# V quantised in a pipe over three engines, and K's parts and the ternary weights turned by the DMA crossbar

## What is computed

```python
kv = (cond @ Wkv + bkv).reshape(1, -1, 2, H, hd)      # cond: 4096 rows x 512, H = 16 heads of 32
k, v = kv[:, :, 0], kv[:, :, 1]
k = fq_sym(k, axis=-1)      # s = max|k| / 127 over a head's 32 columns; round(k / s) * s
v = fq_sym(v, axis=2)       # s = max|v| / 127 over all 4096 keys, for each column
# later: attn = softmax(q k^T), quantised to 0..255; out = attn v; projection; gated sum
# feed-forward: two products with weights w1, w2 that are round(w / mean|w|) clipped to -1..1
```

## Time and profile before

| | |
|---|---|
| three runs | 2114.99 us median, 2111.75 to 2115.88 |
| the profiled execution | 2113.4 us, of which the profiled span is 2111.6 |
| PE busy | 1680.1 us, 80% of the span |
| DVE | 1832.0 us, 87% |
| ACT | 1374.8 us, 65% |
| POOL | 1393.8 us, 66% |
| mean granted TensorE clock | 0.917 of full speed |

### The profile page before, as it was taken

The page is one execution under the profiler, slowest core; times in us unless marked ns, Lnnn a source line. Parts: engine busy times, 40 slices in busy tenths (PEclk is TensorE's granted clock), DMA queues, the critical chain, the costliest instruction groups (busy, mean ns, idle before and its releaser), DMA issues. The chain is left out here.

```text
span 2111.6 us, 38599 instructions
## 1 busy us (share of the span) xinstructions
PE 1680.1 (80%) x14322; PEld 855.0 (40%) x14336; DVE 1832.0 (87%) x2532; ACT 1374.8 (65%) x1294; POOL 1393.8 (66%) x1693
## 2 busy tenths in 40 slices
PE   7899999158888888888888878878878878753546
PEld 3455555014444444444444434434434434322223
DVE  6798888869999989989989989979989956648887
ACT  4344444147877877877877877867877852387771
POOL 0022222438998988988988988988988985134431
PEclk9999999559999999999989999989999988886878
DMA  6533333247767777677667677677677663000001
GB/s 214 174 90 105 105 104 89 80 107 128 134 115 128 130 114 133 124 121 132 123 116 130 124 114 131 114 123 133 115 127 129 111 117 124 20 0 0 20 20 41
DMA packets 596911, 224.99 MB, mean 107 GB/s; under 512 B 537089, under 2 KB 570369, under 8 KB 594817
## 3 DMA queue, kind: packets, MB, share of 16 engines
q1 hardware_dynamic: 596160, 221.04, 51.9%
q0 software_dynamic: 576, 1.57, 0.2%
HBM read 65.27 MB, written 23.07 MB: 42 GB/s over the span
## 5 line engine op out<-in xcount | busy, mean ns | idle before, releaser
L750 DVE TENSOR_SCALAR_CACHE_REDUCE att_scaled<-att_scores,layer_nsq 128x1536 f32<-128x1536 f32 (+1 forms) x768 | 1202.6, 1634 | 91.9 <-PE att_scores L724 89.6
L796 ACT ACTIVATE att_pairs<-att_scaled,att_bias_row 128x4096 uint8<-128x4096 f32 x256 | 950.3, 3712 | 301.1 <-POOL att_bias_row L763 205.6
L772 POOL CAST att_probsT<-att_pairsT 128x1024 bf16<-128x1024 uint8 x1024 | 1022.7, 1042 | 82.1 <-DMA att_pairsT<-att_pairs 68.7
L724 PE MATMUL att_scores<-att_k_head,att_q_head 96*128 96x512 bf16 x2048 | 601.1, 398 | 154.1 <-DVE att_scaled L750 84.9
L711 PE MATMUL att_ps_o<-att_k_head,att_q_head 96*128 96x512 bf16 x1536 | 434.6, 394 | 80.4 <-ACT layer_o_sum L788 80.2
L724 PEld LDWEIGHTS att_scores<-att_k_head,att_q_head 96*128 96x128 bf16 x2048 | 167.2, 100 | 427.9 <-DVE att_scaled L750 242.5
L733 PEld LDWEIGHTS att_ps_o<-att_v_head,att_probsT 128*128 128x128 bf16 x8192 | 245.3, 96 | 67.0 <-issue 8.4
L711 PEld LDWEIGHTS att_ps_o<-att_k_head,att_q_head 96*128 96x128 bf16 x1536 | 147.7, 100 | 290.1 <-ACT layer_o_sum L788 119.7
L733 PE MATMUL att_ps_o<-att_v_head,att_probsT 128*128 128x32 bf16 x8192 | 246.4, 177 | 0.2 <-POOL att_probsT L772 0.2
L556 POOL TENSOR_TENSOR kv_rest<-kv_kq,kv_parts 128x512 f32<-128x512 f32 x32 | 37.9, 1185 | 195.7 <-ACT kv_parts L538 188.4
L760 POOL TENSOR_SCALAR att_low_row<-att_low 128x1 f32<-128x1 f32 x256 | 93.4, 365 | 61.2 <-DVE att_scaled L750 61.1
(11 more groups left out here) (143 smaller groups left out, 1683.6 us busy)
## 6 DMA issues: line engine op xcount, KB each, us to landing
k_parts<-kv_k_stage SPq DMA_DIRECT2D x16, 768.0 KB, 5.1
att_k_head<-k_parts SPq DMA_DIRECT2D x16, 768.0 KB, 6.5
q_w_in<-in_L_ffn_w_dram SPq DMA_DIRECT2D x32, 256.0 KB, 3.2
kv_weights_ctx_in<-in_ctx_dram SPq DMA_DIRECT2D x32, 256.0 KB, 4.1
kv_weights_w_in<-in_L_ffn_w_dram SPq DMA_DIRECT2D x32, 256.0 KB, 2.6
att_q_head<-q_ints SPq DMA_DIRECT2D x48, 128.0 KB, 6.3
q_x_in<-in_x_dram SPq DMA_DIRECT2D x16, 256.0 KB, 2.9
v_ints<-kv_v_int SPq DMA_DIRECT2D x4, 1024.0 KB, 5.2
```

The source lines that it names most:

```text
L724: last = pe.matmul(buffer[:, x:x + 512], q_head[slot][:, at:at + P], k_head[slot][:, STARTS[j] + x:STARTS[j] + x + 512], start=True, stop= ...
L750: dve.tensor_scalar(scaled[u][:, STARTS[j]:STARTS[j] + WIDTHS[j]], scores[(g * NCH + j) % 2][:, 0:WIDTHS[j]], kept["nsq"][:, g:g + 1], Non ...
L772: pool.tensor_copy(probsT[g % C_BUFS][:, parity * HALF + first:parity * HALF + first + HALF // 2, :] .rearrange("p k q -> p (k q)"), turne ...
L796: act.activation(pairs[g % R_BUFS][:, :].bitcast(U8).rearrange("p (c two) -> p two c", two=2), scaled[u][:, :].rearrange("p (two c) -> p t ...
```

## The change

It does three things, all within `project_keys_values`:

1. K's parts are turned by one DMA transpose per tile. `parts` has four slots for each head, the fourth filled with zeros, so that a tile is 128x2048 and each head's block of 128 columns comes out as 128 partitions. SP issues it in step k+4; the 16 TensorE transposes, their PSUM buffers and ScalarE's copies are gone. ScalarE's first cast of a tile waits until the crossbar has turned the tile that was in that buffer before.
2. The ternary weights are turned by one DMA transpose per piece, straight into `w1T` or `w2T`. The three steps that make them move from VectorE to GpSimd, between the `rest` and the third part of its step. SP's and GpSimd's programs are written out without loops. On VectorE the running minimum of V takes the place of the maximum of its negative.
3. V's integers: VectorE multiplies V by the inverse step in eight pieces of four tiles, ScalarE copies each to int8, GpSimd casts that to bf16 in head order into `v_int`.

```diff
-        parts = [c.sb(f"parts{i}", [P, H, 3, D], BF16) for i in range(2)]
+        parts = [c.sb(f"parts{i}", [P, H, 4, D], BF16) for i in range(2)]
+        PART = 4
+        v_round = [c.sb(f"v_round{i}", [P, PART, C], I8) for i in range(2)]
...
             @block.sync
+                sp.wait_ge(parts_padded, 2)
+                for g in range(KT + 6):
+                    if 2 <= g < KT:
+                        sp.wait_ge(ctx_turned, g - 1)
+                        sp.dma_start(ctx_in[g % 2][:, :], ctx_tiles[:, g, :]).then_inc(ctx_loaded[g % 2], 16)
...
+                        sp.wait_ge(tern_ready, g - 1)
+                        sp.dma_start(w_in[g % 2][:, :], piece).then_inc(w_loaded[g % 2], 16)
+                    if live(g - 2, KT):
+                        w = g - 2
...
+                        sp.wait_ge(tern_ready, w + 1)
+                        sp.dma_start_transpose(into, tern[w % 2][:, :]).then_inc(w_turned[w % 2], 16)
+                    if live(g - 4, KT):
+                        k = g - 4
+                        sp.wait_ge(parts_ready, k + 1)
+                        after(sp, k_stored[k // 2 % 2], 16 * (k // 4))
+                        sp.dma_start_transpose(k_stage[k // 2 % 2][:, :, k % 2 * P:(k % 2 + 1) * P],
+                                               parts[k % 2][:, :, :, :].rearrange("p h a d -> p (h a d)")).then_inc(parts_turned[k % 2], 16)
+                    if live(g - 5, KT) and (g - 5) % 2:
+                        k = (g - 5) // 2
+                        for i in range(2):
+                            sp.wait_ge(parts_turned[i], 16 * (k + 1))
...
             @block.tensor
-                    if live(g - 2, KT):
-                        after(pe, tern_ready, g - 1)
...
-                            last = pe.transpose(ps_w[s % 2][:, k, :], tern[s % 2][:, k * P:(k + 1) * P], kept["identb"][:, :])
...
-                    if live(g - 3, KT):
...
-                                last = pe.transpose(ps_t[half][0:3 * D, h % (H // 2), :],
-                                                    parts[r][:, h, :, :].rearrange("p a d -> p (a d)"), kept["identb"][:, :])
...
             @block.scalar
-                            act.copy(k_stage[r // 2][:, half * H // 2:(half + 1) * H // 2, (r % 2) * P:(r % 2 + 1) * P],
-                                     ps_t[half][0:3 * D, :, :]).then_inc(parts_kept, 1)
...
                         after(act, kv_math, NPER * (g - 1))
-                        after(act, parts_turned, 2 * (g - 3) if live(g - 3, KT) else 0)
+                        if live(g - 4, KT):
+                            act.wait_ge(parts_turned[r], 8 * (g - 4 - r) + 16)
                         act.copy(parts[r][:, :, 0, :], heads(kq[r][:, :])).then_inc(hi_ready, 1)
...
+                for i in range(KT // PART):
+                    act.wait_ge(v_norm, i + 1)
+                    after(act, v_int_ready, i - 1)
+                    act.copy(v_round[i % 2][:, :, :], v_raw[:, i * PART:(i + 1) * PART, :]).then_inc(v_rounded, 1)
...
             @block.gpsimd
                         pool.tensor_tensor(heads(rest[r][:, :]), heads(kq[r][:, :]), parts[r][:, :, 0, :],
                                            ALU.subtract).then_inc(rest_ready, 1)
+                    if live(g - 1, KT):
+                        r = (g - 1) % 2
+                        pool.wait_ge(w_loaded[r], 8 * (g - 1 - r) + 16)
+                        pool.tensor_scalar(w_in[r][:, :], w_in[r][:, :], kept["w_scale"][:, r:r + 1], ROUND,
+                                           ALU.mult, ALU.add).then_inc(w_math, 1)
+                        pool.wait_ge(w_math, 2 * g - 1)
+                        pool.tensor_scalar(w_in[r][:, :], w_in[r][:, :], ROUND + 1.0, ROUND - 1.0, ALU.min, ALU.max).then_inc(w_math, 1)
+                        pool.wait_ge(w_math, 2 * g)
+                        if live(g - 3, KT):
+                            pool.wait_ge(w_turned[r], 16 * ((g - 3) // 2 + 1))
+                        pool.tensor_scalar(tern[r][:, :], w_in[r][:, :], -ROUND, 1.0, ALU.add, ALU.mult).then_inc(tern_ready, 1)
                     if live(g - 2, KT):
                         after(pool, mid_ready, g - 1)
                         pool.tensor_tensor(parts[r][:, :, 2, :], heads(rest[r][:, :]), parts[r][:, :, 1, :],
                                            ALU.subtract).then_inc(parts_ready, 1)
...
+                    pool.tensor_copy(v_int[grp % 2][:, :, first:first + PART, :],
+                                     v_round[i % 2][:, :, :].rearrange("p j (h d) -> p h j d", d=D)).then_inc(v_int_ready, 1)
...
             @block.vector
-                        dve.scalar_tensor_tensor(v_low[:, :], v_tile, -1.0, v_low[:, :], ALU.mult, ALU.max).then_inc(kv_math, 1)
+                        dve.tensor_tensor(v_low[:, :], v_tile, v_low[:, :], ALU.min).then_inc(kv_math, 1)
...
-                    for j in range(GRP):
-                        dve.tensor_scalar(v_int[i % 2][:, :, j, :], heads(v_raw[:, i * GRP + j, :]), ROUND, -ROUND,
-                                          ALU.add, ALU.add).then_inc(v_int_ready, 1)
+                for i in range(KT // PART):
+                    block_ = v_raw[:, i * PART:(i + 1) * PART, :]
+                    dve.tensor_tensor(block_, block_, v_inv[:, :].unsqueeze(1).to_broadcast([P, PART, C]), ALU.mult).then_inc(v_norm, 1)
```

More of the change, by code:

```diff
@@ L12 @@
 U8 = mybir.dt.uint8
+I8 = mybir.dt.int8
 ALU = mybir.AluOpType
@@ L437, in _ @@
             def _(sp):
[L438 to L451, removed]
@@ L493, in step @@
                         last.then_inc(k_ready, 1)
-                    if live(g - 3, KT):
[L496 to L500, removed]
-                                last = pe.transpose(ps_t[half][0:3 * D, h % (H // 2), :],
-                                                    parts[r][:, h, :, :].rearrange("p a d -> p (a d)"), kept["identb"][:, :])
-                            last.then_inc(parts_turned, 1)
                 pipelined(pe, KT, UNROLL, 4, step)
@@ L514, in step @@
                         act.copy(inT[s % 2][:, :, :], ps_in[s % 2][:, :, :]).then_inc(ctx_kept, 1)
-                    if live(g - 4, KT):
-                        r = (s - 4) % 4
-                        if r % 2 == 0 and live(g - 8, KT):
-                            after(act, k_stored[r // 2], 4 * (g - r) - 16)
-                        for half in range(2):
-                            after(act, parts_turned, 2 * (g - 4) + half + 1)
-                            act.copy(k_stage[r // 2][:, half * H // 2:(half + 1) * H // 2, (r % 2) * P:(r % 2 + 1) * P],
-                                     ps_t[half][0:3 * D, :, :]).then_inc(parts_kept, 1)
-                    if live(g - 2, KT):
-                        r = (s - 2) % UNROLL
-                        after(act, w_turned, g - 1)
-                        if r % 2:
-                            act.copy(kept["w2T"][:, r // 2 * CT:(r // 2 + 1) * CT, ds((g - 2 - r) * (P // UNROLL), P)],
-                                     ps_w[s % 2][:, :, :]).then_inc(w_kept, 1)
-                        else:
-                            act.copy(kept["w1T"][:, :, ds((g - 2) * (P // 2), P)], ps_w[s % 2][:, :, :]).then_inc(w_kept, 1)
                     if live(g - 2, KT):
@@ L560, in step @@
                                            ALU.subtract).then_inc(parts_ready, 1)
-                pipelined(pool, KT, UNROLL, 4, step)
-                pool.wait_ge(v_math, 3)
-                for i in range(KT // GRP // 2, KT // GRP):
-                    block_ = v_raw[:, i * GRP:(i + 1) * GRP, :]
-                    pool.tensor_tensor(block_, block_, v_inv[:, :].unsqueeze(1).to_broadcast([P, GRP, C]), ALU.mult).then_inc(v_norm, 1)
+                for i in range(2):
+                    pool.memset(parts[i][:, :, 3, :], 0.0).then_inc(parts_padded, 1)
+                for g in range(KT + 2):
+                    step(g)
+                for i in range(KT // PART):
+                    grp, first = i * PART // GRP, i * PART % GRP
+                    pool.wait_ge(v_rounded, i + 1)
+                    after(pool, v_stored[grp % 2], 16 * (grp // 2))
+                    pool.tensor_copy(v_int[grp % 2][:, :, first:first + PART, :],
+                                     v_round[i % 2][:, :, :].rearrange("p j (h d) -> p h j d", d=D)).then_inc(v_int_ready, 1)
             @block.vector
```

52 lines of the change are left out of this document (19 added, 33 removed).

## The result

The changed kernel takes 2165.19 us (median of 4, 2160.05 to 2168.19) against 2114.26 us before: ratio 1.0237, 95% interval 1.0216 to 1.0258. It is slower by 51 us between the medians, where the forecast had 47. The profiled execution took 2166.59 us with a span of 2164.8 us, 53.2 more than the span of before.

The account below looks back on a forecast made before the run. The tile loop was taken as TensorE-bound before, and bound by a ring of waits through the crossbar transposes after: 2113.4 + 51 (ring) - 1 (start) + 2 (tile 30's end) - 5 (V) = 2160.4 us, range 2106 to 2218.

Parts of the forecast that it names:

- the ring: K/V tile loop: first part, remainder, weight steps, SP, two transposes, next first part; 10.5 us against 8.73, +51 us.
- The issue of the weight transpose: SP's issue of the 128x512 transpose in each tile: 0.74 us, bounds 0.33 and 1.97.
- GpSimd's weight steps: Three GpSimd tensor_scalar of 128x512 per tile: 0.61 us each and 0.09 before each, 2.10 in all.
- Port: In the tile loop, GpSimd's steps and VectorE's two-input steps shut each other out: 0.5 us a tile, bounds 0 and 2.8.
- Queueing and hand-overs: In the loop: cast to remainder 0.78, SP's wake 0.2, parts' transpose 4.3 plus 0.3 queueing, landing to ScalarE 0.1 us.
- Start, end of tile 30, V: Around the loop: first products earlier, -1 us; weight steps inside tile 30's end, +2; V's new pipe, -5.
- the third rival: Tile loop: ring of 12 us and TensorE's clock falls, 2205 to 2290 us; single falls mostly taken by slack; chance 0.13.
- TensorE's own work: Tile loop without both turns: 0.61 + 3.65 + 3.60 = 7.86 us of TensorE a tile.
- What the prediction said of the context load: Tile loop: not in the ring; lands 3.5 to 6.5 us after going out, so TensorE finishes before the ring comes round.
- The rival of the port that does not matter: Port no matter to one-input steps: ring 10.0 us, V gains 16, total 2135 us; chance 0.15.
- The rival of a ring that does not bind: Tile loop: ring 8.6 us or less, TensorE binds at about 8.1, total 2091 us, faster; chance 0.15.
- block by block: Crossbar turns a tile's 16 blocks one after the other: ring of 21 us or more, over 2450 us; chance 0.02.

## Why the prediction was right

2160.4 was forecast, in a range from 2106 to 2218, and 2165.2 measured. The mechanism was right. That the number is so near is in part luck: against the profiled execution (2166.6) the ring cost 10 us more than forecast, the start 1 more, V gained 2 more, and the untouched stages were 2.9 shorter, which leaves 6 of the 11. The steps:

- **The ring.** Right, and it is the whole result: ScalarE waits for the crossbar in the changed kernel, the period moves with each link that is taken out or put in (1.50 for 1.67, 0.55 for 0.74), and it opens with one DMA issued earlier. Forecast 10.5, measured 10.84; +51 against +61.4 us.
- **The issue of the weight transpose** is the term that was mis-sized. A quarter of the way between a plain issue and that of 16 blocks gave 0.74; it takes 1.19 to 1.20 at the median. The time does not go by blocks from a plain issue on: a plain issue takes 0.33, four blocks 1.19, sixteen 1.92 at the median. It stands in every turn of the ring: 29 x 0.45 = 13 us. With the 0.1 before the next issue, and a few issues that take up to 3.15 us, the link is 1.42 at the mean.
- **GpSimd's weight steps** were forecast at 0.61 from casts of other widths. Undisturbed they take 0.68, 0.61 and 0.62; the first, with a scale from SBUF, is the dearer.
- **Port.** 0.5 us were forecast. In the loop the means of the remainder and the three weight steps are 1308 (1152 at the least), 980 (680), 740 (614) and 670 (619) ns: 0.16 + 0.30 + 0.13 + 0.05 = 0.64.
- **Queueing and hand-overs** were too dear: 4.4 us from issue to landing at the median (4.6 forecast), 0.03 from ternary tile to SP (0.2 forecast), 0.69 from cast to remainder (0.78). They cancel about half of the three errors above; 0.3 us a tile are left.
- **Start, end of tile 30, V.** -0.1 (forecast -1), +2.1 (+2), -7.3 (-5). V gained more mostly since a cast of 2048 columns takes 1.89, not 2.1 (8 x 0.21 = 1.7 us).
- **TensorE's clock.** It fell in the loop (0.88 at the mean). From 150 us on about every second tile has an idle time of 3.9 to 6.6 us ahead of the context's turn, and its next eight products take 4.6 to 6.0 us instead of 3.60. TensorE's slack took that up, as the third rival said of single falls: `kq` was ready at least 2.8 us before every cast. With the order of one DMA changed and the same work the clock is 0.96, and of ScalarE's waits for the crossbar one of 0.3 us is left.
- **TensorE's own work** was put at 7.86 us a tile, by adding durations of rows that overlap (306.78 lies before 303.29 + 3.65 in rows 4). Where it waits for nothing in the kernel with the transpose first, its turns of the context start 7.31 us apart (256.45, 263.76). The sum does not hang on it, but the price of a ring that does not bind does: there VectorE, at 7.8, comes ahead of it.
- **What the prediction said of the context load** held in the changed kernel: it lands, and TensorE and VectorE do their work, before the ring comes round. That it binds as soon as the ring is open, it did not say, and two of my later expectations (four buffers, weights on VectorE) were missed by it.
- **The rival of the port that does not matter** fell: casts and products take turns. The rival of a ring that does not bind fell; among its low ends it needed a plain issue, 0.33 us, for the weight transpose, which takes 1.19. So did block by block: 16 blocks land in 4.4 us and four in 3.0 here as well, where the Trainium skill (VectorE: DVE Perf Modes, section The three transpose paths) gives 1309 ns for one.
- The rule of the Trainium skill on the port (SBUF — State Buffer, section Who interferes with whom), that a VectorE instruction contends with GpSimd's reads when both its inputs lie in SBUF and, outside its two-port modes, not when one at most does, is borne out beyond what rows of before could show: 3942 against 1892 ns for GpSimd's one-input cast, and 1893 with VectorE's second operand in PSUM.

## What to carry to other kernels

Idle time of an engine is slack only if nothing that it does lies on the ring of waits that sets the period. When a step moves to an idle engine, follow who waits for it, who waits for that, and whether it comes back to the same engine one tile later; the sum of that ring, DMA issue and landing included, is the new period. DMAs that one engine issues in program order are tied together though they have nothing to do with each other: put the DMA that frees a buffer ahead of waits for later data, and don't put a small urgent load right behind a big store. And when the ring is open, look for the next one before you name the new period.

## What the runs showed of the hardware

- A crossbar transpose of 128x512 two-byte values holds SP for 1.19 us and lands 3.0 us after its start at the median; 128x2048 hold it for 1.92 and land after 4.4. In the kernel with the transpose issued first, the issue of 128x2048 takes 3.09 at the median and up to 6.09 us; what it then waits for, no run shows.
- A cast of GpSimd with one input and a step of VectorE with two inputs in SBUF shut each other out (3942 against 1892 ns a cast, 26.39 against 17.67 us for eight products); with one of VectorE's operands in PSUM neither loses.
- A context load of 128x512 issued right behind the 768 KB store landed 5.6 to 6.7 us after its issue, the others 2.6 to 4.0; with the store moved ahead by two DMAs and a wait none took more than 3.7.
- A wait of 3.8 us of TensorE for data cost 1.2 us more in the products that followed it (4.84 against 3.60).
